# A blocked feed-forward layer with layer norm and projection: the first stage reordered with groups outermost, row means taken from a running sum, the root taken on 128x4 values, and matmul operands placed and read in one way

## The chip, the cores and the metric

One core of a Trainium2 chip. The metric is the device time of one execution in microseconds (us), the median of three runs of the kernel. One more execution was taken with the hardware profiler; all rows below are from it.

## What is computed

For x of shape 4 x 1024 x 1024 (4 batches, 1024 tokens, D = 1024 features in 8 groups of 128):

```python
xr = x.reshape(B, T, 8, 128)
h  = gelu(einsum('btel,elf->btef', xr, W1) + b1)      # W1: 8 x 128 x 512
y  = (einsum('btef,efl->btel', h, W2) + b2).reshape(B, T, D)   # W2: 8 x 512 x 128
scale, shift = split(silu(emb) @ emb_W + emb_b, 2)    # emb: 4 x 1024, emb_W: 1024 x 2048
hn = layernorm(y, ln_g, ln_b) * (1 + scale) + shift   # mean and variance over D
out = x + silu(hn) @ out_W + out_b                    # out_W: 1024 x 1024
```

All is float32. The large products are made of three matmuls in the format fp32r each: an operand is split in a rounded part ("hi") and the rest ("lo"), and hi\*hi, lo\*hi and hi\*lo are added in PSUM.

## The kernel before

**Stage A** makes y. A block is 1024 tokens (one batch), an item is one group of one block; the blocks are the outer loop (`body`, the two in the middle as a loop on the device) and the 8 groups the inner one. An item has 4 chunks of 128 hidden features. For a chunk, `first` makes six matmuls 128x128x512 (three products for two halves of the tokens) from `W` and `xT_hi`/`xT_lo` into one of two PSUM slots, the ring. ScalarE applies gelu into `g_raw` (L469), VectorE rounds to `g_hi` (L612) and subtracts to `g_lo` (L614), and `second` (six more matmuls, L792) adds into `y_psum`. TensorE issues `first` of chunk m + 2 ahead of `second` of chunk m. Per item ScalarE also rounds the next x to `xT_hi` (L465) and copies y with its bias to `y_stage` (L497), which SyncE's queue stores in `y_scratch`; VectorE makes `xT_lo` (L607). In the first block ScalarE rounds each group's W1 and W2, and GpSimd subtracts for the low parts (L387) and adds each `y_stage` to a sum for the first window (L405), in one queue. All eight groups' weights stay in SBUF. In the middle blocks ScalarE and GpSimd split out_W in the same way, and TensorE makes the eight float32 products of the conditioning (`embed`, L807).

**Stage B** works on eight windows of 512 tokens. For a window TensorE makes 4 x 48 matmuls (`project`, L892): four row tiles, eight groups, three products, two halves. Meanwhile the next window is normed: VectorE adds y over the groups and splits the sum (`group_sum`, L689 to L697), TensorE averages over partitions with a matrix of 1/D (`mean_of_sum`, L799 and L800), VectorE subtracts (L708), ScalarE squares (L565), the squares go the same way through `group_sum` and `mean_of_sum`, ScalarE takes the root and VectorE the reciprocal on 128x512 (L747), then come the product (L713), silu (L550), rounding (L719) and subtraction (L721), and after each row tile PSUM + `res` (L703). GpSimd adds `out_b` to `res` (L450), two buffers deep.

The first window is normed inside the last block of stage A: GpSimd subtracts the mean (L431), adds the squares (L436) and multiplies (L443), eight times each, and VectorE takes the reciprocal in three pieces (L669). Its silu, rounding and subtraction (`Y0_PARTS`) lie at the seam of the stages.

SBUF tensors lie behind one another, and three unused ones (`gap0`, `gap1`, `gap2`) shift them. By the declared sizes and the program's start at byte 16,512 of a partition, `W`, `oW_hi`, `oW_lo` and all `s_hi`, `s_lo` begin at byte 448 modulo 512, `xT_hi`, `xT_lo`, `g_hi`, `g_lo` at 192, `ones_r` at 352, `sum_hi` and `sum_lo` at 384. In stage A the moving operand (x or gelu) is read backwards:

```python
def from_the_end(h):
    return slice((h + 1) * BANK - 1, h * BANK - 1 if h else None, -1)
```

Of the kernel before, what the change touches and what calls it, by code (L numbers as in the profile page):

```python
# [15 lines left out]
def cond_ffn_program(nc, x, xT, vectors, W1, W2, emb_W, out_W, out_b, out):  # L16
# [5 lines left out]
    TA = T  # L22
    NA = B * T // TA
    TB = BANK
    H = TA // TB
    NB = B * T // TB
    SB = TB // P
    K = G * C
    assert L == P and D == G * L and TA == 2 * BANK and D == 2 * BANK and G % 2 == 0 and C == 4

    y_scratch = nc.dram_tensor("y_scratch", [NB, P, G, TB], F32, kind="Internal").ap()

# [10 lines left out]
    with ExitStack() as ctx:  # L43
        def sb(name, shape, dt=F32, scope=ctx):
            return scope.enter_context(nc.sbuf_tensor(name, shape, dt))
# [5 lines left out]


        sb("gap0", [P, 80])
        oW_hi = sb("oW_hi", [P, G, D], F32R)
        oW_lo = sb("oW_lo", [P, G, D], F32R)
        ident = sb("ident", [P, P])
        cols = sb("cols", [P, ROWS])
        ones_r = sb("ones_r", [P, P], F32R)
        eps = sb("eps", [P, 1])
        stat = sb("stat", [P, TB])  # L60

        sum_hi = sb("sum_hi", [P, TB], F32R)
        sum_lo = sb("sum_lo", [P, TB], F32R)
        cond_silu = sb("cond_silu", [P, KE, 32])
        cond_now = sb("cond_now", [P, 2, 32])
        emb_rows = sb("emb_rows", [P, BANK])
        sq_sum = emb_rows
        emb = sb("emb", [P, NE, B])
        mod_a = sb("mod_a", [P, B, G])
        mod_c = sb("mod_c", [P, B, G])  # L70
        mod_t = sb("mod_t", [P, B, G])
        sb("gap2", [P, 48])


        with ExitStack() as a:

            W = sb("W", [P, G, 4, FF], F32R, a)
            sb("gap1", [P, 64], F32, a)
            xT_hi = sb("xT_hi", [P, 2, TA], F32R, a)
            xT_lo = sb("xT_lo", [P, 2, TA], F32R, a)  # L80
            g_hi = sb("g_hi", [P, 2, TA], F32R, a)
            g_lo = sb("g_lo", [P, 2, TA], F32R, a)
            g_raw = sb("g_raw", [P, 2, TA], F32, a)
            xT_raw = sb("xT_raw", [P, 2, TA], F32, a)
            y_stage = sb("y_stage", [P, 2, TA], F32, a)
            wraw = sb("wraw", [P, 2, 2 * FF], F32, a)
            assert D == 2 * FF == KE * P


        with ExitStack() as b:  # L90
            yb0 = sb("yb0", [P, G, TB], F32, b)
            s_lo0 = sb("s_lo0", [P, G, TB], F32R, b)
            s_hi0 = sb("s_hi0", [P, G, TB], F32R, b)
            sq = sb("sq", [P, G, TB], F32, b)
            yb1 = sb("yb1", [P, G, TB], F32, b)
            s_hi1 = sb("s_hi1", [P, G, TB], F32R, b)
            s_lo1 = sb("s_lo1", [P, G, TB], F32R, b)
            res = sb("res", [P, 2, D], F32, b)
            out_b_all = sb("out_b_all", [P, D], F32, b)
        yb = (yb0, yb1)  # L100
        s_hi = (s_hi0, s_hi1)
        s_lo = (s_lo0, s_lo1)
        W1_HI, W1_LO, W2_HI, W2_LO = range(4)
        HG = G // 2

        squares = wraw[:].rearrange("p s (g t) -> p (s g) t", g=2)

        sp_waits = sem("sp_waits")
# [3 lines left out]
        ident_ready = sem("ident_ready")  # L112
        vec_landed = sem("vec_landed")
        ones_set = sem("ones_set")
        ones_ready = sem("ones_ready")

        wraw_landed = [sem(f"wraw_landed{s}") for s in range(2)]
        w1_landed = sem("w1_landed")
        w_hi_done = sem("w_hi_done")
        w_split0 = sem("w_split0")  # L120
# [5 lines left out]
        cond_now_ready = sem("cond_now_ready")  # L126
# [7 lines left out]
        x0_landed = [sem(f"x0_landed{h}") for h in range(2)]  # L134
        x0_hi = sem("x0_hi")
        x0_lo = sem("x0_lo")
# [4 lines left out]
        ghi_done = sem("ghi_done")  # L141
        glo_done = sem("glo_done")
        s2_done = sem("s2_done")
        y_psum_free = sem("y_psum_free")
        y_staged = sem("y_staged")
        y_stored = [sem(f"y_stored{s}") for s in range(2)]


        y0_landed = sem("y0_landed")
        y0_sum = sem("y0_sum")  # L150
        y0_split = sem("y0_split")
# [4 lines left out]
        y0_var = sem("y0_var")  # L156
        y0_std = sem("y0_std")
        y0_rstd = sem("y0_rstd")
# [7 lines left out]
        tree = sem("tree")  # L166
        sum_split = sem("sum_split")
        stat_psum = sem("stat_psum")
        centred = sem("centred")
        squared = sem("squared")  # L170
        std_done = sem("std_done")
        rstd_done = sem("rstd_done")
# [6 lines left out]
        res_landed = [sem(f"res_landed{s}") for s in range(2)]  # L179
        res_biased = sem("res_biased")  # L180
        out_ready = sem("out_ready")
        out_stored = [sem(f"out_stored{s}") for s in range(2)]


        def ring(s):
            return psum[:, 2 * s:2 * s + 2, :].rearrange("p b n -> p (b n)")

        def y_psum(s):
            return psum[:, 4 + 2 * s:6 + 2 * s, :].rearrange("p b n -> p (b n)")

        proj = [ring(0), ring(1)]
        mean_ps = psum[:, 4]
        var_ps = psum[:, 5]

        PERIOD = 16
        AT_ROUND = (2, 5)
        AT_LOAD = (6, 10)
        AT_EMB = (10, 14)
        K_EMB = [p + k for p in range(0, K, PERIOD) for k in AT_EMB]
        E_PER_BLOCK = len(K_EMB)
        K_TURN = 2
# [767 lines left out]
```

## Time and profile before

| | |
|---|---|
| median of 3 runs | 783.93 us (783.43 to 785.17) |
| the profiled execution | 777.46 us, of which the span from the first to the last instruction is 775.7 us |
| TensorE matmuls | 736.8 us busy, 95% of the span, 3172 instructions |
| VectorE | 638.9 us, 82% |
| ScalarE | 332.6 us, 43% |
| GpSimd | 215.7 us, 28% |
| DMA | 101.65 MB, mean 131 GB/s |
| granted TensorE clock | 0.998 over the span |

A matmul's record is longer than the distance to the next one (they are pipelined), so what a matmul costs is read from the distance of their starts. Idle time of the other engines counts only where TensorE waits for it.

### The profile page before, as it was taken

Reading aid. Unit: us, or ns where it says so; the run is one execution under the profiler, and the core shown is the slowest. Engines: PE = TensorE matmul, PEld = TensorE weight load, DVE = VectorE, ACT = ScalarE, POOL = GpSimd, SP = SyncE. Lnnn points to the kernel's source line nnn. Section 1 sums busy time; section 2 is a strip of 40 time slices with the busy share of each in tenths; the row PEclk is TensorE's granted clock in tenths of the full one; section 3 lists DMA queues with packets and bytes.
Section 4 is the critical chain, followed back from the end, with each engine's and each line's share of the span. In section 5 each row is a group of like instructions: output and inputs, shape, how many; then the busy total and the mean of one; then the engine's idle time right before and its main releaser. Section 6 shows DMA issues by size and latency. Waiting matters only on the chain.

```text
span 775.7 us, 8764 instructions
## 1 busy us (share of the span) xinstructions
PE 736.8 (95%) x3172; PEld 584.3 (75%) x3172; DVE 638.9 (82%) x491; ACT 332.6 (43%) x327; POOL 215.7 (28%) x107
## 2 busy tenths in 40 slices
PE   7989899999999999989988999999999999999998
PEld 5767687787787877856666878888787887878886
DVE  6898989878797887798999798989889899988511
ACT  5656466565574755556561313324131332404100
POOL 2343525022040220374342312231323121232121
PEclk9999999999999999999999999999999999999999
DMA  5343324535344443341245344242534324132321
GB/s 165 103 142 97 121 95 145 195 136 190 127 146 160 162 162 109 112 160 55 82 145 207 109 157 168 83 190 81 190 108 189 120 90 193 57 109 109 109 86 77
DMA packets 32110, 101.65 MB, mean 131 GB/s; under 512 B 2896, under 2 KB 6992, under 8 KB 29904
## 3 DMA queue, kind: packets, MB, share of 16 engines
q1 hardware_dynamic: 31408, 100.73, 36.6%
q10 hardware_dynamic: 672, 0.52, 0.2%
q8 instruction: 19, 0.31, 0.2%
q14 instruction: 11, 0.09, 0.0%
HBM read 67.69 MB, written 33.55 MB: 131 GB/s over the span
## 4 chain that ended last, share of the span: by engine, by line
PE 66%; DVE 14%; issue 13%; POOL 4%; ACT 1%; DMA 1%; SPq 0%; DVEq 0%; POOLq 0%; ACTq 0%
PE psum L892 34%; PE psum L778 14%; PE psum L792 14%; DVE g_hi L612 3%; DVE sq L689 2%; DVE sq L691 2%; DVE sum_lo L697 2%; POOL W L387 2%; PE psum L905 1%; POOL stat L405 1%; DVE g_lo L614 1%; PE psum L807 1%; DMA yb<-y_scratch 1%; DVE xT_lo L607 1%; PE psum L799 1%
## 5 line engine op out<-in xcount | busy, mean ns | idle before, releaser
L469 ACT ACTIVATE g_raw<-psum,cols 128x1024 f32<-128x1024 f32 x128 | 142.4, 1114 | 145.7 <-PE psum L778 110.6
L614 DVE TENSOR_TENSOR g_lo<-g_raw,g_hi 128x1024 fp32r<-128x1024 f32 x128 | 182.9, 1429 | 4.4
L450 POOL TENSOR_TENSOR res<-res,out_b_all 128x1024 f32<-128x1024 f32 x32 | 91.4, 2858 | 273.1 <-DMA res<-in_x 273.1
L892 PE MATMUL psum<-oW_hi,s_hi 128*128 128x512 f32 x496 | 153.4, 390 | 0.0
L892 PE MATMUL psum<-oW_lo,s_hi 128*128 128x512 f32 x496 | 153.2, 390 | 0.0
L892 PE MATMUL psum<-oW_hi,s_lo 128*128 128x512 f32 x496 | 153.2, 390 | 0.0
L778 PE MATMUL psum<-xT_hi,W 128*128 128x512 f32 x508 | 142.0, 403 | 9.6 <-POOL W L387 8.8
L612 DVE CAST g_hi<-g_raw 128x1024 fp32r<-128x1024 f32 x128 | 111.2, 869 | 41.2 <-PE psum L792 36.3
L792 PE MATMUL psum<-g_hi,W 128*128 128x512 f32 x512 | 140.8, 398 | 1.3 <-DVE g_hi L612 1.3
L778 PEld LDWEIGHTS psum<-xT_hi,W 128*128 128x128 f32 x508 | 95.0, 190 | 41.5 <-issue 18.0
L792 PEld LDWEIGHTS psum<-g_hi,W 128*128 128x128 f32 x512 | 96.0, 188 | 25.4 <-DVE g_hi L612 2.4
L892 PEld LDWEIGHTS psum<-oW_hi,s_hi 128*128 128x128 f32 x496 | 93.7, 189 | 19.7
L892 PEld LDWEIGHTS psum<-oW_lo,s_hi 128*128 128x128 f32 x496 | 93.4, 188 | 19.6
L892 PEld LDWEIGHTS psum<-oW_hi,s_lo 128*128 128x128 f32 x496 | 93.4, 188 | 19.5
L792 PE MATMUL psum<-g_lo,W 128*128 128x512 f32 x256 | 82.2, 403 | 7.5 <-DVE g_lo L614 7.3
L565 ACT ACTIVATE sq<-yb 128x2048 f32<-128x2048 f32 x14 | 26.9, 1919 | 134.7 <-DVE yb L708 134.7
L778 PE MATMUL psum<-xT_lo,W 128*128 128x512 f32 x254 | 80.7, 400 | 0.6 <-DVE xT_lo L607 0.6
L703 DVE TENSOR_TENSOR res<-psum,res 128x1024 f32<-128x1024 f32 x31 | 37.9, 1221 | 40.1 <-PE psum L892 40.1
L550 ACT ACTIVATE yb<-yb,mod_c,mod_a 128x512 f32<-128x512 f32 x64 | 47.0, 805 | 42.3 <-DVE yb L713 42.1
L792 PEld LDWEIGHTS psum<-g_lo,W 128*128 128x128 f32 x256 | 46.9, 188 | 24.0 <-DVE g_lo L614 13.8
L387 POOL TENSOR_TENSOR oW_lo<-wraw,oW_hi 128x512 f32 x16 | 29.8, 1884 | 124.7 <-ACT oW_hi L539 124.7
L778 PEld LDWEIGHTS psum<-xT_lo,W 128*128 128x128 f32 x254 | 47.9, 189 | 12.7 <-DVE xT_lo L607 1.2
(85 smaller groups left out, 598.6 us busy)
## 6 DMA issues: line engine op xcount, KB each, us to landing
y_scratch<-y_stage SPq DMA_DIRECT2D x32, 512.0 KB, 3.1
res<-in_x SPq DMA_DIRECT2D x32, 512.0 KB, 3.3
xT_raw<-in_xT SPq DMA_DIRECT2D x31, 512.0 KB, 4.7
out<-res SPq DMA_DIRECT2D x31, 512.0 KB, 2.6
yb<-y_scratch SPq DMA_DIRECT2D x7, 2048.0 KB, 8.8
wraw<-in_emb_W SPq DMA_DIRECT2D x8, 1024.0 KB, 4.8
wraw<-in_out_W SPq DMA_DIRECT2D x8, 512.0 KB, 4.6
wraw<-in_W SPq DMA_DIRECT2D x14, 256.0 KB, 3.7
```

The lines of the kernel that those rows point to most:

```text
L387: nc.gpsimd.tensor_tensor(lo, raw, hi.bitcast(F32), ALU.subtract).then_inc(pw_split, 1)
L450: nc.gpsimd.tensor_tensor(res[:, t % 2], res[:, t % 2], out_b_all[:], ALU.add).then_inc(res_biased, 1)
L469: nc.scalar.activation(g_raw[:, k % 2], ring(slot), ACT.Gelu, bias=cols[:, R_B1 + k:R_B1 + k + 1]).then_inc(gelu_done, 1)
L550: return nc.scalar.activation(yb[s][:, g], yb[s][:, g], ACT.Silu, scale=mod_a[:, b, g:g + 1], bias=mod_c[:, b, g:g + 1])
L565: nc.scalar.activation(sq[:, half], yb[s][:, half], ACT.Square).then_inc(squared, 1)
L612: nc.vector.tensor_copy(g_hi[:, s], g_raw[:, s]).then_inc(ghi_done, 1)
L614: nc.vector.tensor_tensor(g_lo[:, s], g_raw[:, s], g_hi[:, s].bitcast(F32), ALU.subtract).then_inc(glo_done, 1)
L689: nc.vector.tensor_tensor(sq[:, 0:4], src[:, 0:4], src[:, 4:8], ALU.add).then_inc(tree, 1)
L703: nc.vector.tensor_tensor(res[:, t % 2], proj[t % 2], res[:, t % 2], ALU.add).then_inc(out_ready, 1)
L778: mm = nc.tensor.matmul(ring(slot)[:, h * BANK:(h + 1) * BANK], W[:, g, w, cut], v[:, g % 2, from_the_end(h)], start=(n == 0), stop=(n == 2))
L792: mm = nc.tensor.matmul(y_psum(g % 2)[:, h * BANK:(h + 1) * BANK], W[:, g, w, cut], v[:, k % 2, from_the_end(h)], start=(c == 0 and n == 0 ...
L892: mm = nc.tensor.matmul(proj[t % 2][:, h * BANK:(h + 1) * BANK], v[:, g, cut], w[:, g, h * BANK:(h + 1) * BANK], start=(g == 0 and n == 0) ...
```

## The change

- **Order.** Stage A runs over items with the groups outside: group 0 for the four blocks, group 1 for the four, up to group 5; then for each block its groups 6 and 7. All loops are written out, none runs on the device. `W` holds three groups' weights instead of eight. The loads and splits of W and out_W are one list (`LOADS`), spread over items 0 to 22 (`PREP_ITEM`), with two splits of 512 columns on GpSimd in each such item. GpSimd no longer adds up y.
- **Means.** VectorE keeps a running sum `acc` of y over the groups for all tokens, one instruction per item (`add_up`), PSUM and `acc` in, `acc` out. The mean is one float32 matmul of `ones` with `acc`.
- **Variance and root.** The sum of squares is turned by four float32 matmuls with one column (`variance`) to 128x4, ScalarE's root and VectorE's reciprocal work on 128x4, and four transposes (`spread`) bring the result back to 128x512 in PSUM, where VectorE's product reads it. For the first window ScalarE copies it to `stat`.
- **Gelu.** Two of an item's four chunks are rounded to `g_hi` by ScalarE, right behind the gelu. In stage B the rounding of silu (`s_hi`) goes to ScalarE too.
- **Placement.** Each SBUF tensor that a matmul reads has an address that is 0 modulo 512, and all are read forward.
- `res` has four buffers instead of two; those of the first two row tiles are loaded before the last item ends. The conditioning's weights have a buffer of their own.

```diff
+    ORDER = [(g, t) for g in range(G - 2) for t in range(NT)] + [(g, t) for t in range(NT) for g in (G - 2, G - 1)]
...
+    PREP_ITEM = [None, 0, 1, 2, 3, 5, 6, 7, 9, 11, 13, 15, 17, 19, 21, 22]
...
+    Y0_MEAN_AT = (Y0_ITEM + 2, 0)
+    Y0_SQ_AT = [(Y0_ITEM + 2, 3), (Y0_ITEM + 3, 1), (Y0_ITEM + 3, 2), (Y0_ITEM + 4, 0)]
+    Y0_VAR_AT = (Y0_ITEM + 4, 3)
+    Y0_RSTD_AT = (Y0_ITEM + 5, 1)
...
+        BASE = 33 * 512
...
+    def act_rounds(m):
+        return m % C in (3, 0)
...
+                if act_rounds(m):
+                    act.wait_ge(gelu_done, m + 1)
+                    if m >= 2:
+                        act.wait_ge(s2_done, m - 1)
+                    nc.scalar.copy(g_hi[:, m % 2], g_raw[:, m % 2]).then_inc(ghi_act, 1)
...
+            def add_up(n):
+                g, t = ORDER[n]
+                dve.wait_ge(s2_done, C * n + C)
...
+                    nc.vector.scalar_tensor_tensor(acc[:, t], y_psum(n), bias, acc[:, t], ALU.add, ALU.add
+                                                   ).then_inc(acc_done, 1)
...
+            def variance(ps, sums):
+                for j in range(SB):
+                    mm = nc.tensor.matmul(ps[:, j:j + 1], sums[:, j * P:(j + 1) * P], ones[:, 0:1],
+                                          start=True, stop=True)
+                return mm
+
+            def spread(ps):
+                for j in range(SB):
+                    mm = nc.tensor.transpose(ps[:, j * P:(j + 1) * P], rstd[:, j:j + 1].to_broadcast([P, P]), ident[:])
+                return mm
...
+                at_mean, at_var, at_rstd = ((0, 3), (2, 1), (2, 5)) if i == 0 else ((0, 0), (1, 0), (1, 4))
...
+                            if i == 0:
+                                pe.wait_ge(y_staged, N)
+                                pe.wait_ge(acc_done, N)
...
+                            nc.tensor.matmul(mean_ps, ones[:], acc[:, n, (i + 1) % 2 * TB:((i + 1) % 2 + 1) * TB],
+                                             start=True, stop=True).then_inc(mean_done, 1)
...
+                            pe.wait_ge(tree, 3 * i + 3)
+                            variance(var_ps, stat).then_inc(var_done, 1)
...
-                                              v[:, g % 2, from_the_end(h)],
...
+                        mm = nc.tensor.matmul(ps[:, half], W[:, g % 3, w, cut], v[:, n % 2, half],
```

On VectorE the last `add_up` (item 31) stands behind all `Y0_PARTS`. The item of the first window's last group is item 25, so its mean stands at item 27, its squares at items 27 to 29, its variance at (29, 3) and its root at (30, 1), the second number being the chunk.

## Rows read from the trace of the kernel before

**Rows 1.** The page, part 1: busy us, share of the span, instructions.

```profile
PE 736.8 (95%) x3172; PEld 584.3 (75%) x3172; DVE 638.9 (82%) x491; ACT 332.6 (43%) x327; POOL 215.7 (28%) x107
```

**Rows 2.** Timeline, TensorE in stage A: start us, us, instruction, count.

```profile
300.89 1.10 PE L778 MATMUL psum<-xT_hi,W 128*128 128x512 f32 x4
...
303.69 1.10 PE L778 MATMUL psum<-xT_hi,W 128*128 128x512 f32 x4
```

**Rows 3.** Timeline, TensorE, start of stage B and its first mean.

```profile
403.32 0.62 PE L892 MATMUL psum<-oW_hi,s_hi 128*128 128x512 f32 x2
...
416.47 0.61 PE L892 MATMUL psum<-oW_hi,s_lo 128*128 128x512 f32 x2
420.85 0.54 PE L799 MATMUL psum<-sum_hi,ones_r 128*128 128x512 f32 x1 [3.77 <-DVE sum_lo L697]
...
421.62 1.06 PE L892 MATMUL psum<-oW_hi,s_hi 128*128 128x512 f32 x2
422.47 1.06 PE L892 MATMUL psum<-oW_lo,s_hi 128*128 128x512 f32 x2
```

**Rows 4.** The stretch behind the wait of rows 3, columns as in rows 5.

```profile
420.80:424.80 4.00, 3.95 (x10) 3.16 (x11) 2.94 (x2) 0.62 (x1) 0.00 (x0) 0.57 0.00 0
```

**Rows 5.** Stretches: us, busy (x) of PE, PEld, DVE, ACT, POOL; granted clock; DMA.

```profile
307.00:403.30 96.30, 86.53 (x353) 64.60 (x353) 87.08 (x75) 55.33 (x54) 46.02 (x25) 1.00 0.28 97
403.30:775.70 372.40, 358.17 (x1565) 294.05 (x1564) 293.93 (x175) 96.17 (x99) 91.43 (x32) 1.00 0.35 130
```

**Rows 6.** Waits of TensorE over the span: us in total, times, longest us.

```profile
PE psum L799 <- DVE sum_lo L697: 11.1, 6, 3.8
PE psum L778 <- POOL W L387: 8.8, 6, 1.6
```

**Rows 7.** Timeline, TensorE at the last wait for GpSimd's weights.

```profile
92.61 0.63 PE L792 MATMUL psum<-g_lo,W 128*128 128x512 f32 x2
94.82 0.94 PE L778 MATMUL psum<-xT_hi,W 128*128 128x512 f32 x3 [1.58 <-POOL W L387]
```

**Rows 8.** VectorE's sum of PSUM and SBUF: shortest, median, longest in ns.

```profile
L703 DVE TENSOR_TENSOR res<-psum,res x31: 1217/1220/1225, 426.3 to 761.7; 128x1024 f32<-128x1024 f32 x31
```

**Rows 9.** Groups: line, engine, operation, count, busy us, mean ns, idle before.

```profile
L469 ACT ACTIVATE g_raw<-psum,cols 128x1024 f32<-128x1024 f32 x128 | 142.4, 1114 | 145.7 <-PE psum L778 110.6
...
L465 ACT CAST xT_hi<-xT_raw 128x1024 fp32r<-128x1024 f32 x31 | 32.5, 1049 | 4.5 <-ACT y_stage L497 2.2
```

**Rows 10.** Timeline, GpSimd at the end of stage A and the seam.

```profile
380.51 15.50 POOL L443 TENSOR_TENSOR yb<-yb,stat 128x512 f32<-128x512 f32 x8 [21.84 <-DVE stat L669]
414.78 5.38 POOL L450 TENSOR_TENSOR res<-res,out_b_all 128x1024 f32<-128x1024 f32 x2 [18.77 <-DMA res<-in_x]
```

**Rows 11.** The low part of gelu, two SBUF inputs: shortest, median, longest in ns.

```profile
L614 DVE TENSOR_TENSOR g_lo<-g_raw,g_hi x128: 1224/1226/2293, 10.6 to 401.5; 128x1024 fp32r<-128x1024 f32 x128
```

**Rows 12.** Timeline, TensorE around one float32 product of the conditioning.

```profile
199.25 0.63 PE L792 MATMUL psum<-g_lo,W 128*128 128x512 f32 x2
199.81 1.07 PE L807 MATMUL psum<-wraw,cond_now 128*32 128x512 f32 x8
200.81 1.20 PE L778 MATMUL psum<-xT_hi,W 128*128 128x512 f32 x4
```

**Rows 13.** Timeline around the four float32 transposes.

```profile
306.02 0.63 PE L792 MATMUL psum<-g_lo,W 128*128 128x512 f32 x2
...
306.49 0.60 PE L855 MATMUL psum<-ident,emb_rows 128*128 128x128 f32 x4
...
306.84 0.95 PE L778 MATMUL psum<-xT_hi,W 128*128 128x512 f32 x3
```

**Rows 14.** Timeline, VectorE in a window of stage B.

```profile
556.16 4.48 DVE L708 TENSOR_TENSOR yb<-yb,psum 128x2048 f32<-128x2048 f32 x2 [0.83 <-PE psum L800]
...
566.22 0.69 DVE L693 TENSOR_TENSOR stat<-sq 128x512 f32<-128x512 f32 x1
```

**Rows 15.** Timeline, VectorE, its first work behind the seam.

```profile
411.16 2.29 DVE L689 TENSOR_TENSOR sq<-yb 128x2048 f32<-128x2048 f32 x1
```

More of the change, by code:

```diff
@@ L377, in _ @@
+            for s in range(4):
+                sp.wait_ge(out_stored[s], 16 * (QN // 4 + (s == (QN - 1) % 4)))
         @block.gpsimd
@@ new lines, in round_raw @@
+            def round_raw(j, h):
+                kind, g = LOADS[j]
+                half = slice(h * FF, (h + 1) * FF)
+                if kind == "W" and g >= 3:
+                    act.wait_ge(s2_done, C * (LAST_ITEM[g - 3] + 1))
+                landed = sum(q % 2 == j % 2 for q in range(1, j + 1))
+                act.wait_ge(wraw_landed[j % 2], 32 * landed)
+                nc.scalar.copy(W[:, g % 3, 2 * h] if kind == "W" else oW_hi[:, g, half], wraw[:, j % 2, half]
+                               ).then_inc(aw_hi_done, 1)
@@ L822, in _, with take @@
[L822 to L831 removed]
+            def take(u):
+                if u in EARLIER:
+                    kind, j = EARLIER[u]
                     if kind == "S":
[L833 removed]
+                        pe.wait_ge(gelu_done, j + 1)
@@ new lines, in take, with first @@
+                return ring(u)
+            def first(m, low_part=None):
+                n, c = divmod(m, C)
+                g = ORDER[n][0]
+                cut = slice(c * P, (c + 1) * P)
+                ps = take(("S", m))
+                for k, (w, v) in enumerate(((W1_HI, xT_hi), (W1_LO, xT_hi), (W1_HI, xT_lo))):
+                    if k == 2 and low_part is not None:
+                        pe.wait_ge(xlo_done, low_part)
+                    for h in range(2):
+                        half = slice(h * BANK, (h + 1) * BANK)
+                        mm = nc.tensor.matmul(ps[:, half], W[:, g % 3, w, cut], v[:, n % 2, half],
+                                              start=(k == 0), stop=(k == 2))
+                mm.then_inc(s1_done, 1)
@@ new lines, in second @@
+            def second(m):
+                n, c = divmod(m, C)
+                g = ORDER[n][0]
+                cut = slice(c * P, (c + 1) * P)
+                pe.wait_ge(ghi_act if act_rounds(m) else ghi_dve, ROUNDED[m])
+                for k, (w, v) in enumerate(((W2_HI, g_hi), (W2_LO, g_hi), (W2_HI, g_lo))):
+                    if k == 2:
+                        pe.wait_ge(glo_done, m + 1)
+                    for h in range(2):
+                        half = slice(h * BANK, (h + 1) * BANK)
+                        mm = nc.tensor.matmul(y_psum(n)[:, half], W[:, g % 3, w, cut], v[:, m % 2, half],
+                                              start=(c == 0 and k == 0), stop=(c == C - 1 and k == 2))
+                mm.then_inc(s2_done, 1)
```

1028 lines of the change are left out of this document (455 added, 573 removed).

## The prediction

> **What bounds the kernel now.** I read the page first: TensorE is busy for 95% of the span, VectorE for 82% [rows 1]. So the question is what one matmul costs and where TensorE is kept from the next. The timeline gives the first. In the middle of stage A twelve matmuls take 303.69 - 300.89 = 2.80 us, 233.3 ns each [rows 2]. In stage B 58 matmuls take 416.47 - 403.32 = 13.15 us, 226.7 ns each [rows 3]. There are 1536 in each stage. A floor comes from the stretch behind 421 us, where the granted clock is down: two matmuls take 422.47 - 421.62 = 0.85 us, 427 ns each, one column per pulse of 1.2 GHz [rows 3, 4]; at 2.4 GHz that is 213 ns, and no distance of these matmuls is shorter.
>
> Then the losses, from the stretches and the waits. The last two blocks of stage A, 307 to 403.3, hold 353 matmuls; at 233.3 ns they need 82.4 us of 96.3, so 13.9 us are lost there [rows 5], while VectorE is busy for 87 us and GpSimd norms the first window. In the first block TensorE waits six times for GpSimd's half of the weights, 8.8 us [rows 6]. In stage B it waits six times for the split sum, 11.1 us [rows 6]: once 3.77 us [rows 3], behind which the granted clock is 0.57 for 4.0 us, near the level of 1.2 GHz, and ten matmuls take 4.00 instead of 2.27 us [rows 4]; five times for 7.3 us in all. The reader should see that TensorE has no single bottleneck behind it, only these terms.
>
> **The change part by part**, in terms of the span of 775.7 us. The profiled execution took 777.46 us, 0.8% less than the median of 783.93; I carry the difference over to the median as it is.
>
> *Placement and direction.* In stage B the two operands begin at one byte modulo 512 (448) and are read forward: 226.7 ns. In stage A they begin at 448 and 192, and the moving one is read backwards: 233.3 ns [rows 2, 3]. Stage A gets what stage B has, so I give it stage B's distance: 1536 x 6.6 ns = 10.1 us less. Stage B stays, since it had the one place already; only the place itself moves (448 to 0). Bounds: nothing (0), and the floor of 213 ns for all 3072, which is 31 us for stage A and 21 us for stage B.
>
> The Trainium skill speaks against a gain here: "TensorE: Matmul & The Clock Gate", part 2, says that TensorE has two independent SBUF read ports and that loading the next weights takes nothing from the running matmul, so that a matmul's distance would depend on its columns alone. The two distances above, for equal columns, don't agree with it; by the rule this term would be zero and the sum 786 us.
>
> *Order of the groups.* GpSimd's share of a group's weights is now due every fourth item instead of every item, and its queue no longer holds the sum of y that stood ahead of it. The six waits go. One of them costs 94.82 - 92.61 less two distances (0.47) = 1.74 us where the wait is 1.58 [rows 7], and the matmul behind it comes 0.08 us later; so 8.8 + 6 x 0.25 = 10.3 us less. Behind it nothing else is late: GpSimd's two pieces of 1.9 us an item are few against 10.9 us.
>
> *Gelu rounding and running sum.* VectorE loses two roundings an item and gets `add_up`, which reads PSUM and one SBUF tensor like L703 and should take 1.22 us [rows 8]; its free load per item stays about 8.3 to 8.6 us of 10.9. ScalarE gets two casts of 1.05 us on top of four gelus of 1.11, y and x [rows 9]: 4.5 + 1.1 + 1.05 + 2.1 = 8.7 us, 9.9 with a weight rounding. Both hide under TensorE's 48 x 0.2267 = 10.9 us. A gelu's low part is due, counted from the end of its `first`, after four sets of six matmuls and the first four of the fifth: 5.4 + 0.9 = 6.3 us. It is ready after one set, which must have left the buffer (1.6 with the signals), a cast (1.05 and 0.1) and a subtraction (1.23): 4.0. That leaves 2.3 us, so the extra hop to ScalarE is covered too. If that cover were gone, each cast would cost what it is late.
>
> *Norming of the first window.* GpSimd still does its 23 instructions in stage A (15.50 us for eight, 1.94 each [rows 10]), and a VectorE instruction that reads two SBUF tensors then takes up to 2.29 instead of 1.23 us [rows 11], while the sum from PSUM takes 1.22 at its shortest and 1.23 at its longest [rows 8]. Before, nine VectorE instructions an item are exposed to that, now seven. The 13.9 us of rows 5 shrink by two ninths: 3.1 us less. The squares at item 28 stand close together, and ScalarE's queue can be held there by GpSimd with gelus behind it; I take that as part of what remains. TensorE's own part grows by the 2.2 us of one window, next.
>
> *Short products.* A float32 mean replaces two fp32r matmuls (0.46 us). The float32 product of the conditioning with as many columns costs 200.81 - 199.25 less two distances = 1.1 us, and 0.1 behind it [rows 12]: 1.2. Four transposes cost 306.84 - 306.02 less two distances = 0.35, and 0.1: 0.45 [rows 13]. `variance` isn't in the trace: four float32 matmuls of one column, two records each as in rows 12, hence eight weight loads. Low end: the transposes' distance, 0.35 / 4 = 0.09 us each, 0.7 and 0.1 at each side, 0.9. High end: 584.3 / 3172 = 0.18 us for a weight load [rows 1] plus a start of its own, 1.8. I take 1.5, nearer to the loads, since nothing long hides them. Per window 1.2 + 0.45 + 1.5 = 3.15 against 0.92 before: 2.2 us more, seven times 15.6 in stage B and once 2.2 in stage A.
>
> *Waits in stage B.* The five short waits go: 7.3 + 5 x 0.2 = 8.3 us less. In their place: from the mean to the end of the squares' sum VectorE and ScalarE need 566.91 - 556.16 = 10.8 us [rows 14], and `variance` stands eight groups behind the mean, 8 x 1.36 = 10.9 us. That is a tie; I take 0.3 us in each of six windows, 1.8 more (0 to 2 each, if GpSimd meets a sum). The reciprocal of 3.4 us and the slow product leave the chain, but the next window's operands were in time before, so that is worth nothing.
>
> *The seam.* Before: 420.85 - 416.47 - 0.45 = 3.9 us, and 1.7 for the clock [rows 3, 4], 5.7. After: the mean of window 1 waits for `add_up` of item 31, which VectorE does behind all of `Y0_PARTS`; these ended 411.16 - 403.32 = 7.8 us after the first projection [rows 3, 15]. Now 1.2 are added by ScalarE's last cast ahead of the silus, 1.2 by `add_up`, 0.2 for the signals, and some 3 because GpSimd's products and its first sums with `out_b`, 2.7 us each [rows 10], now fall into this stretch. That is 13.4 us, and TensorE has four groups of 1.36 to do before it: 8.0 lost, and 1.7 if the clock falls again. 9.7 - 5.7 = 4.0 more.
>
> Sum: - 10.1 - 10.3 - 3.1 + 2.2 + 15.6 - 8.3 + 1.8 + 4.0 = - 8.2 us. 783.93 - 8.2 = **775.7 us**.
>
> **The rivals.**
> 1. *The short products and the seam are cheap.* `variance` at its low end saves 0.6 x 8 = 4.8 us, GpSimd staying out of the seam and the clock staying up 4.7, the tie in stage B 1.8: 775.7 - 11.3 = 764 us. For it: loads are pulled ahead in all of stage B. Against it: one column hides no load.
> 2. *The place itself counts.* At 0 modulo 512 both stages come down toward the floor, say half of the 13.4 ns above it: 3072 x 6.7 ns = 21 us less, 755 us; the whole would be 735. For it: the rest over the floor is unexplained. Against it: 448 and 448 gave no better than 226.7.
> 3. *Slower: stage A's distance does not move.* If the 233.3 ns belong to stage A's traffic and not to place and direction, 10.1 us don't come: 775.7 + 10.1 = 786 us. It decides when the new distance is above 226.7 + 8.2 / 1.536 = 232.0 ns. For it: ScalarE and VectorE write these very tensors. Against it: the distance stays 233.3 whether they are idle or busy. (The two-port rule of "TensorE: Matmul & The Clock Gate" in the Trainium skill, part 2, would give this case.)
> 4. *Slower: the hop to ScalarE.* If the 64 casts make TensorE wait, 0.13 us each is enough to eat the gain (8.2 / 64); at 0.3 us each it is 19 us, 795 us. For it: ScalarE's queue is in order, and x, y and weights stand in it. Against it: 2.3 us of slack.
>
> **How the numbers follow.** Forecast (769 to 782): 0.42. Rival 1: 0.21. Rival 2, fully or in part: 0.11. Rival 3: 0.14. Rival 4, or the first window's chain costing as much: 0.12. A difference under 0.2% (1.6 us) can't be told from none in this kernel. Faster: all of the first three, 0.74; within 0.2%: 0.07, taken from the edges of the forecast and rival 3; slower: 0.19. The range leaves out most of rival 2 and the far half of rival 4: 757 to 789.
>
> **What the profile after would show.** Distances of 226 to 228 ns in stage A confirm the placement; 233 refute it. No wait of L778's successor for GpSimd in the first quarter. The float32 mean as two records 0.43 us apart; `variance` between 0.9 and 1.8 us from the projection before to the one behind. A gap of some 7 us in the first row tile of stage B, and a granted clock near one half behind it. VectorE's `add_up` at 1.22 us. GpSimd's squares and ScalarE waiting for its subtraction at item 28. The prediction is wrong if stage A waits steadily for ScalarE, if the variance costs over 2 us, or if the matmul distance leaves 226 to 234.

## The result, and the profile after

The kernel after the change takes 794.08 us (median of four runs, 791.87 to 795.2), the kernel before 783.68 us (782.93 to 785.17). The ratio is 1.0127, 95% interval 1.0099 to 1.0155: slower, where I had forecast 775.7 us and faster. The profiled execution took 794.72 us, with a span of 792.9. The one of the kernel before took 777.46, which is 6.2 us under that kernel's median, while this one is at its median. So the two traces lie 17.2 us apart and the medians 10.4: some 7 us of the differences between them below are no loss of the change, and nothing here says which.

The page, part 1, of the kernel after, answers to [rows 1]. VectorE has lost 150 us of work and ScalarE has gained 86, as the change intends; TensorE keeps its share of 95%, in a span that is 17 us longer.

```profile
PE 751.7 (95%) x3252; PEld 597.4 (75%) x3252; DVE 489.3 (62%) x393; ACT 418.1 (53%) x413; POOL 165.6 (21%) x91
```

The timeline of TensorE in stage A answers to [rows 2]. From the first of these two lines to the last are twelve matmuls: 153.46 - 150.74 = 2.72 us, 226.7 ns each, where it was 233.3.

```profile
150.74 1.07 PE L682 MATMUL psum<-xT_hi,W 128*128 128x512 f32 x4
...
153.46 1.07 PE L682 MATMUL psum<-xT_hi,W 128*128 128x512 f32 x4
```

The waits of TensorE over the span, as in [rows 6]:

```profile
PE psum L682 <- DVE xT_lo L525: 13.4, 11, 4.4
PE psum L728 <- DVE W L512: 5.8, 1, 5.8
PE psum L822 <- DVE acc L548: 4.5, 1, 4.5
PE psum L682 <- ACT g_raw L400: 2.6, 2, 1.6
PE psum L696 <- DVE g_lo L537: 2.2, 3, 1.0
PE psum L778 <- DVE res L608: 1.9, 1, 1.9
PE psum L682 <- ACT stat L462: 1.8, 1, 1.8
PE psum L778 <- DVE s_hi L599: 1.8, 1, 1.8
PE psum L778 <- DVE s_lo L601: 1.6, 1, 1.6
```

The reader should see that both waits of [rows 6] are gone, the six for GpSimd's weights and the six for `sum_lo`, and that a new one leads the list: eleven times TensorE waits for `xT_lo`, the low part of the next item's input. The wait for `W` at L728 is the start of the kernel, which was there before.

To find where the time went I cut each trace at three points of TensorE's timeline: its first matmul, the mean of the first window, and the first projection. In each piece I count the 512-column matmuls of the two layers and of the projection, and take off 226.7 ns for each. What is left is the loss of the piece; for the kernel before, the longer distance of stage A counts as loss here. "Predicted" applies the terms of the prediction to the losses of the kernel before: 31.9 - 7.9 - 10.3, then 17.4 - 2.2 - 3.1 + 2.2, then 24.1 + 15.6 - 8.3 + 1.8 + 4.0.

| us | first matmul | first mean | first projection | span | loss to the mean | mean to projection | stage B |
|---|---|---|---|---|---|---|---|
| before | 5.8 | 309.7 (1200 matmuls) | 403.3 (336) | 775.7 | 31.9 | 17.4 | 24.1 |
| predicted | | | | 767.5 | 13.7 | 14.3 | 37.2 |
| after | 5.8 | 328.6 (1308) | 408.0 (228) | 792.9 | 26.3 | 27.8 | 36.7 |

Stage B is where I had put it, 12.6 us worse against 13.1 predicted. Stage A should have gained 21.3 us (49.3 to 28.0) and lost 4.8 (54.1): between these traces the whole miss is there, 12.6 us ahead of the mean and 13.5 behind it. In medians the miss is 18.4 us (794.08 against 775.7).

A part of the two losses behind the first mean is the clock. In the kernel after, the granted clock is 0.50, which is the level of 1.2 GHz, in five stretches of 27 us together (columns as in [rows 5]):

```profile
338.30:341.70 3.40, 3.40 (x10) 2.62 (x9) 0.73 (x1) 1.26 (x2) 0.00 (x0) 0.50 0.00 0
369.00:379.20 10.20, 9.39 (x26) 7.74 (x27) 4.31 (x4) 3.44 (x4) 0.00 (x0) 0.50 0.00 0
410.00:416.80 6.80, 6.01 (x14) 4.75 (x15) 6.70 (x8) 0.21 (x1) 2.39 (x2) 0.50 0.42 161
423.60:427.00 3.40, 3.40 (x9) 2.34 (x8) 2.59 (x2) 0.27 (x1) 0.00 (x0) 0.50 0.91 381
468.00:471.40 3.40, 3.40 (x8) 1.98 (x7) 0.50 (x2) 0.00 (x0) 0.00 (x0) 0.50 1.00 288
```

Fifty of the long matmuls (512 columns) start in them. Each takes 427 ns there instead of 226.7, so by this estimate the slow clock costs 10.0 us, 5.2 between mean and projection and 4.8 in stage B. In the kernel before it is one stretch, 421.1 to 424.5, with seven of them, 1.4 us. The prediction had put the clock at 1.7 us, in the seam alone.

### The profile page after: what moved, and what is told of

Its sections match the earlier page's. It is cut to its first block, busy times and chain, and to the rows that moved or that the text cites. A ratio compares the mean times of both kernels' runs of the same rounds, so it can differ in the third digit from the quotient of the medians.

```text
span 792.9 us, 8091 instructions
## 1 busy us (share of the span) xinstructions
PE 751.7 (95%) x3252; PEld 597.4 (75%) x3252; DVE 489.3 (62%) x393; ACT 418.1 (53%) x413; POOL 165.6 (21%) x91
## 4 chain that ended last, share of the span: by engine, by line
PE 78%; DVE 11%; ACT 5%; issue 4%; DMA 2%; POOL 1%; SPq 0%; ACTq 0%; DVEq 0%; POOLq 0%
PE psum L778 39%; PE psum L682 17%; PE psum L696 17%; DVE g_lo L537 4%; DVE xT_lo L525 2%; DVE g_hi L535 2%; PE psum L789 1%; ACT g_raw L400 1%; DMA xT_raw<-in_xT 1%; PE psum L711 1%; PE psum L822 1%; PE psum L704 1%; DVE s_hi L599 1%; ACT yb L470 1%; ACT xT_hi L392 1%
## 5 line engine op out<-in xcount | busy, mean ns | idle before, releaser
L537 DVE TENSOR_TENSOR g_lo<-g_raw,g_hi 128x1024 fp32r<-128x1024 f32 x128 | 178.3, 1393 | 74.1 <-ACT g_hi L406 71.9
L778 PE MATMUL psum<-oW_hi,s_hi 128*128 128x512 f32 x496 | 159.7, 403 | 3.7 <-DVE res L608 1.9
L778 PE MATMUL psum<-oW_hi,s_lo 128*128 128x512 f32 x496 | 155.2, 394 | 1.6 <-DVE s_lo L601 1.6
L682 PE MATMUL psum<-xT_hi,W 128*128 128x512 f32 x508 | 140.0, 398 | 5.0 <-ACT g_raw L400 2.6
L381 POOL TENSOR_TENSOR res<-res,out_b_all 128x1024 f32<-128x1024 f32 x32 | 79.0, 2472 | 281.6 <-DMA res<-in_x 281.6
L682 PE MATMUL psum<-xT_lo,W 128*128 128x512 f32 x254 | 82.4, 406 | 13.4 <-DVE xT_lo L525 13.4
L696 PE MATMUL psum<-g_lo,W 128*128 128x512 f32 x256 | 80.2, 395 | 2.2 <-DVE g_lo L537 2.2
L406 ACT CAST g_hi<-g_raw 128x1024 fp32r<-128x1024 f32 x64 | 67.2, 1050 | 22.4 <-PE psum L696 22.3
L535 DVE CAST g_hi<-g_raw 128x1024 fp32r<-128x1024 f32 x64 | 47.2, 738 | 22.7 <-ACT g_raw L400 17.0
L696 PEld LDWEIGHTS psum<-g_lo,W 128*128 128x128 f32 x256 | 48.5, 190 | 13.8 <-DVE g_lo L537 3.5
```

Of the source, the lines that this page charges most:

```text
L381: nc.gpsimd.tensor_tensor(res[:, q % 4], res[:, q % 4], out_b_all[:], ALU.add).then_inc(res_biased, 1)
L406: nc.scalar.copy(g_hi[:, m % 2], g_raw[:, m % 2]).then_inc(ghi_act, 1)
L535: nc.vector.tensor_copy(g_hi[:, m % 2], g_raw[:, m % 2]).then_inc(ghi_dve, 1)
L537: nc.vector.tensor_tensor(g_lo[:, m % 2], g_raw[:, m % 2], g_hi[:, m % 2].bitcast(F32), ALU.subtract).then_inc(glo_done, 1)
L682: mm = nc.tensor.matmul(ps[:, half], W[:, g % 3, w, cut], v[:, n % 2, half], start=(k == 0), stop=(k == 2))
L696: mm = nc.tensor.matmul(y_psum(n)[:, half], W[:, g % 3, w, cut], v[:, m % 2, half], start=(c == 0 and k == 0), stop=(c == C - 1 and k == 2))
```

## The experiments

**The subtraction of `xT_lo` one chunk earlier.** The waits name `xT_lo`. These are the lines of VectorE's timeline ahead of one of them, in the kernel after, then TensorE's, ScalarE's and GpSimd's:

```profile
24.53 1.23 DVE L537 TENSOR_TENSOR g_lo<-g_raw,g_hi 128x1024 fp32r<-128x1024 f32 x1
26.26 0.69 DVE L535 CAST g_hi<-g_raw 128x1024 fp32r<-128x1024 f32 x1 [0.50 <-ACT g_raw L400]
26.99 2.20 DVE L537 TENSOR_TENSOR g_lo<-g_raw,g_hi 128x1024 fp32r<-128x1024 f32 x1
29.11 1.21 DVE L525 TENSOR_TENSOR xT_lo<-xT_raw,xT_hi 128x1024 fp32r<-128x1024 f32 x1
```

```profile
28.40 1.07 PE L682 MATMUL psum<-xT_hi,W 128*128 128x512 f32 x4
30.37 0.73 PE L682 MATMUL psum<-xT_lo,W 128*128 128x512 f32 x2 [0.91 <-DVE xT_lo L525]
```

```profile
24.18 1.04 ACT L392 CAST xT_hi<-xT_raw 128x1024 fp32r<-128x1024 f32 x1
```

```profile
26.81 1.29 POOL L348 TENSOR_TENSOR W<-wraw,W 128x512 fp32r<-128x512 f32 x1 [2.86 <-ACT W L415]
```

ScalarE has `xT_hi` at 25.22, but VectorE takes the subtraction up only at 29.11, behind the rounding of the item's third chunk, and ends it at 30.32. TensorE has done its four `xT_hi` matmuls by then and starts at 30.37. The low part ahead of it takes 2.20 us instead of 1.23, beside GpSimd's subtraction for the weights; the 0.97 us more are as much as the wait of 0.91. So it is the place in the queue and GpSimd's work next to it that make `xT_lo` late here. The kernel before had `rest_xT` at chunk 0 of an item; the diff has it at chunk 1, one gelu later in the queue. The edit puts it back:

```diff
-                if c == 1 and n + 1 < N:
+                if c == 0 and n + 1 < N:
                     rest_x(n + 1)
```

> The changed kernel with one move: VectorE makes an item's xT_lo one chunk earlier, as the kernel before did. Theory A (a deadline that my prediction overlooked: xT_lo is due 0.9 us into the third chunk's matmuls, but stands behind a low part of gelu that waits for its turn): the waits of TensorE for xT_lo, 13.4 us in the changed kernel, go nearly all, and the time falls by 10 to 15 us, to 779 to 784 us. Rival (the wait only changes its name, since VectorE or ScalarE is the bound in stage A): the time falls by less than 3 us and waits for g_hi or g_lo take its place.

Measured: 776.28 us against 777.76 for the kernel before on that chip, ratio 0.9963, interval 0.9938 to 0.9989; the span is 775.5 us, 17.4 less than after. These are single executions; by the two ratios to the kernel before, 1.0127 and 0.9963, the gain is 1.6%, some 13 us, within the 10 to 15 us expected. The loss to the mean falls from 26.3 to 15.2 us and the one behind it from 27.8 to 21.3; stage B keeps its 36.9. In VectorE's timeline the subtraction now stands in front of the same rounding, and the wait is down to one:

```profile
23.80 1.23 DVE L537 TENSOR_TENSOR g_lo<-g_raw,g_hi 128x1024 fp32r<-128x1024 f32 x1
24.94 1.22 DVE L525 TENSOR_TENSOR xT_lo<-xT_raw,xT_hi 128x1024 fp32r<-128x1024 f32 x1
26.07 0.69 DVE L535 CAST g_hi<-g_raw 128x1024 fp32r<-128x1024 f32 x1
```

```profile
PE psum L682 <- DVE xT_lo L525: 0.6, 1, 0.6
```

So one line of the queue's order is worth some 13 us by the ratios and 17.4 us between the two traces, and the rest of the rewrite is about even with the kernel before: its ratio of 0.9963 lies within the range of the forecast, though not at its middle. The slow clock isn't what the move gives back: 44 long matmuls still start at 0.50 (8.8 us by the same estimate).

**No rounding by ScalarE.** Rival 4 of the prediction said that the hop to ScalarE costs.

```diff
     def act_rounds(m):
-        return m % C in (3, 0)
+        return False
```

> The changed kernel with all roundings of gelu on VectorE, none on ScalarE. If the hop to ScalarE is what makes VectorE late for xT_lo (it waits for ScalarE's cast 71.9 us in all), the waits for xT_lo fall and the time falls by 3 us or more. If the hop is harmless, VectorE, which then has nine instructions an item that read SBUF alone and add_up besides, loses more where GpSimd works: slower by 3 us or more.

Measured: 797.22 us against 777.76, ratio 1.0244 (1.0195 to 1.0293), span 793.9. The loss to the mean is 32.1 us (26.3 after), behind it 28.8, in stage B 30.7 (36.7). `xT_lo` is still waited for, ten times, 11.6 us. The hop isn't the cause: ScalarE's roundings save stage A 6.8 us. They cost stage B 6.0; there the wait for `acc` is 2.4 us instead of 4.5, and what the rest is wasn't taken apart. By the ratios this kernel is slower than the one after by 1.2%, which its span (1.0 us more) doesn't show.

**GpSimd's part of the first norming cut down.** In the first window GpSimd subtracts, sums and multiplies 512 columns; this kernel leaves out all but 8 of them in each instruction except the first sum. The sums are cut in the same way as the two lines shown.

```diff
-nc.gpsimd.tensor_tensor(yb0[:, g], yb0[:, g], stat[:], ALU.subtract)
+nc.gpsimd.tensor_tensor(yb0[:, g, 0:8], yb0[:, g, 0:8], stat[:, 0:8], ALU.subtract)
...
-nc.gpsimd.tensor_tensor(yb0[:, g], yb0[:, g], stat[:], ALU.mult)
+nc.gpsimd.tensor_tensor(yb0[:, g, 0:8], yb0[:, g, 0:8], stat[:, 0:8], ALU.mult)
```

> Leaves out work: GpSimd's subtractions, products and all but the first of its sums for the first window are done on 8 columns of 512, so that window's norm is not computed; the order and the signals stay. Theory B (GpSimd's chain for the first window, with ScalarE's squares waiting in their queue for it and VectorE held by it, costs most of the 28 us that the stretch from the window's mean to the first projection loses): that loss falls under 12 us. Rival (the loss is the late xT_lo and the table loads): it stays above 20 us.

Measured: span 776.2 us, one run of 777.96. The loss to the mean stays (27.5), the one from the mean to the projection falls from 27.8 to 12.2 us, stage B from 36.7 to 34.1. That is just above the 12 us expected, and far from the rival's 20. So more than half of what is lost there comes with the time of GpSimd's instructions, in its chain and in what they do to VectorE, and not with TensorE's own short products, which are unchanged. Of the 15.6 us, some 5.2 are the slow clock, which doesn't fall between mean and projection in this run. The timeline of the kernel after shows the worst of it. First GpSimd, then ScalarE, VectorE and TensorE:

```profile
354.88 5.99 POOL L367 TENSOR_TENSOR yb<-yb,stat 128x512 f32<-128x512 f32 x4
360.82 7.85 POOL L372 TENSOR_TENSOR emb_rows<-emb_rows,squares 128x512 f32<-128x512 f32 x4
```

```profile
358.44 1.06 ACT L453 ACTIVATE squares<-yb 128x1024 f32<-128x1024 f32 x1 [3.90 <-POOL yb L367]
359.40 1.10 ACT L400 ACTIVATE g_raw<-psum,cols 128x1024 f32<-128x1024 f32 x1
```

```profile
365.39 2.17 DVE L537 TENSOR_TENSOR g_lo<-g_raw,g_hi 128x1024 fp32r<-128x1024 f32 x1
367.48 2.28 DVE L525 TENSOR_TENSOR xT_lo<-xT_raw,xT_hi 128x1024 fp32r<-128x1024 f32 x1
```

```profile
369.81 1.22 PE L682 MATMUL psum<-xT_lo,W 128*128 128x512 f32 x2 [4.43 <-DVE xT_lo L525]
```

ScalarE stands 3.90 us in front of a square whose input GpSimd still centres, with a gelu queued behind it. VectorE's next rounding is then late, its subtractions beside GpSimd's sums take 2.2 us instead of 1.23, `xT_lo` stands behind them, and TensorE waits 4.43 us. The stretches of the kernel after (columns as in [rows 5]) show the clock that this costs:

```profile
352.00:384.00 32.00, 24.67 (x90) 18.72 (x89) 17.69 (x14) 18.39 (x19) 16.08 (x10) 0.84 0.10 34
384.00:406.00 22.00, 17.64 (x73) 13.13 (x72) 16.18 (x12) 15.14 (x16) 16.22 (x9) 1.00 0.44 167
406.00:430.00 24.00, 16.14 (x48) 11.63 (x47) 21.10 (x14) 7.20 (x8) 10.10 (x4) 0.79 0.51 197
```

Around and behind this wait the granted clock is 0.50 from 369.0 to 379.2, as shown above: TensorE runs at 1.2 GHz for 10.2 us. With `xT_lo` repaired no wait of that length is left here, and the clock is down for as long all the same, from 353.0 to 363.2, behind waits of 1.61, 0.60, 0.56 and 0.95 us.

**The norming given more items.** Besides the earlier subtraction, groups 5, 6 and 7 go block by block at the end instead of 6 and 7, so the first window is complete four items earlier and its norming has eleven items instead of seven. One load of `PREP_ITEM` moves from item 21 to 20 with it.

```diff
-    ORDER = [(g, t) for g in range(G - 2) for t in range(NT)] + [(g, t) for t in range(NT) for g in (G - 2, G - 1)]
+    ORDER = [(g, t) for g in range(G - 3) for t in range(NT)] + [(g, t) for t in range(NT) for g in (G - 3, G - 2, G - 1)]
...
-    Y0_SQ_AT = [(Y0_ITEM + 2, 3), (Y0_ITEM + 3, 1), (Y0_ITEM + 3, 2), (Y0_ITEM + 4, 0)]
-    Y0_VAR_AT = (Y0_ITEM + 4, 3)
-    Y0_RSTD_AT = (Y0_ITEM + 5, 1)
+    Y0_SQ_AT = [(Y0_ITEM + 2, 3), (Y0_ITEM + 3, 1), (Y0_ITEM + 4, 2), (Y0_ITEM + 5, 0)]
+    Y0_VAR_AT = (Y0_ITEM + 6, 0)
+    Y0_RSTD_AT = (Y0_ITEM + 6, 3)
```

> Besides the earlier xT_lo subtraction, groups 5, 6 and 7 instead of 6 and 7 go block by block at the end, so the first window's mean comes four items earlier and its norming has eleven items left instead of seven (the squares spread over more chunks, the variance and the reciprocal later). Span of the run with only the earlier subtraction: 775.5 us, of which 21.3 us lost against 226.7 ns per matmul between the mean and the first projection, and 36.9 us after it. Theory (this loss is the norming chain through GpSimd run against its deadlines, and its last tail of GpSimd multiplications that collides with the last items and the silus): the 21.3 us shrink to about 8 to 12, and the seam gains 0 to 3 us because the sums of out_b with x then come earlier; span 761 to 768. Rival (the loss is inherent work of the chain on TensorE, ScalarE and VectorE: short products, activation tables, copies): it stays within 3 us of 21.3 and the span above 772.

Measured: 765.3 us against 781.35, ratio 0.9827 (0.978 to 0.9873), span 763.0. Between the mean and the projection, now over 372 matmuls, 13.0 us are lost (21.3 with the early subtraction alone), and stage B loses 32.8 (36.9), 4.1 less where I had allowed for 3. The first is a little more than expected, but far nearer to the theory than to its rival: the same work in more items loses 8.3 us less. Some 3.4 of them are the slow clock, which no longer falls between mean and projection.

**The mean of window 1 one row tile later.** In the kernel after, TensorE waits 4.50 us at the first mean of stage B for the last `add_up`.

```diff
-                at_mean, at_var, at_rstd = ((0, 3), (2, 1), (2, 5)) if i == 0 else ((0, 0), (1, 0), (1, 4))
+                at_mean, at_var, at_rstd = ((1, 0), (2, 3), (2, 7)) if i == 0 else ((0, 0), (1, 0), (1, 4))
```

> The changed kernel with window 1's mean behind the first group of the second row tile (1, 0), its variance at (2, 3) and its root at (2, 7). Theory C (the seam loses because the mean stands where the last add_up can't be ready): the wait of 4.9 us and the slow clock behind it, about 2 us more, go, and the span falls by 5 to 7 us unless window 1's second half comes later. Rival (the chain behind the mean is as late as before and only the place of the wait changes): the wait comes back at the variance or at the start of window 1, and the span falls by under 2 us.

Measured: span 788.7 us, one run of 790.47. Stage B loses 35.6 us, only 1.1 less than after; the other 3.1 us of span lie ahead of the first projection, where this kernel is the same as the one after. The wait for `acc` is gone from the list; the one for `res` has grown from 1.9 us to 7.1 us, in two waits. So a later mean mostly hands the wait on, as the rival said; that it is VectorE's whole queue that is late is argued here, and the next run tests it.

**VectorE's queue in the seam put in order.** VectorE's timeline at the seam of the kernel after, and GpSimd's under it:

```profile
405.37 1.27 DVE L548 SCALAR_TENSOR_TENSOR acc<-psum,cols,acc 128x1024 f32<-128x1024 f32 x1
406.57 1.38 DVE L599 CAST s_hi<-yb 128x512 fp32r<-128x512 f32 x1
407.99 2.75 DVE L601 TENSOR_TENSOR s_lo<-yb,s_hi 128x512 fp32r<-128x512 f32 x1
...
411.11 0.69 DVE L601 TENSOR_TENSOR s_lo<-yb,s_hi 128x512 fp32r<-128x512 f32 x1
...
415.44 2.87 DVE L599 CAST s_hi<-yb 128x1024 fp32r<-128x1024 f32 x1
418.35 3.25 DVE L601 TENSOR_TENSOR s_lo<-yb,s_hi 128x1024 fp32r<-128x1024 f32 x1
421.52 1.27 DVE L548 SCALAR_TENSOR_TENSOR acc<-psum,cols,acc 128x1024 f32<-128x1024 f32 x1
```

```profile
404.33 5.85 POOL L381 TENSOR_TENSOR res<-res,out_b_all 128x1024 f32<-128x1024 f32 x2
414.60 5.91 POOL L381 TENSOR_TENSOR res<-res,out_b_all 128x1024 f32<-128x1024 f32 x2 [4.41 <-DMA res<-in_x]
```

The last running sum, on which the mean waits, stands last, behind two instructions that take 2.87 and 3.25 us beside the sums with `out_b`, instead of 0.69 and 1.23. Besides the earlier `xT_lo`, this kernel moves it up, rounds the last chunk on VectorE, and brings variance and rstd forward:

```diff
-        return m % C in (3, 0)
+        return m % C in (3, 0) and m != M - 1
...
             for n, part in enumerate(Y0_PARTS):
+                if part.start == HG:
+                    dve.wait_ge(y_staged, N)
+                    add_up(N - 1)
                 dve.wait_ge(y0_silu, part.stop)
...
-            add_up(N - 1)
...
-                at_mean, at_var, at_rstd = ((0, 3), (2, 1), (2, 5)) if i == 0 else ((0, 0), (1, 0), (1, 4))
+                at_mean, at_var, at_rstd = ((0, 3), (1, 4), (2, 0)) if i == 0 else ((0, 0), (1, 0), (1, 4))
```

> Besides the earlier xT_lo subtraction, the last chunk of gelu is rounded by VectorE instead of ScalarE, the last running sum is put before the third-to-last part of the first window's s_hi and s_lo in VectorE's queue (behind the last y_stage of ScalarE), and the variance and the rstd of the next window come at row tile 1 group 4 and row tile 2 group 0 instead of row tile 2 groups 1 and 5. Span of the run with only the earlier subtraction: 775.5 us, of which 36.9 us lost after the first projection, its window 0 60.2 us long. Theory (the mean matmul behind row tile 0 group 3 waits for the last running sum, which stands last in VectorE's queue, and window 1 starts late because everything behind that mean is late): the gap of about 5.8 us on TensorE there goes to below 1.5, window 0 takes 50 to 55 us, window 1 about 46.5, and the span is 764 to 770. Rival (VectorE's and GpSimd's total work in the seam bounds it, whatever its order): the wait moves to s_hi or s_lo or to the finish of row tiles, window 0 and 1 together gain less than 2 us, span above 773.

Measured: 770.15 us against 781.35, ratio 0.9881 (0.9836 to 0.9926), span 764.7. The profiled execution is the fastest of the four; the others have spans of 767.7 to 769.1. Stage B loses 26.1 us instead of 36.9; window 0 takes 50.9 us (60.2) and window 1 46.2 (47.6). The wait for `acc` is gone; 1.7 us appear in front of the variance. The same two instructions are still as long beside GpSimd, but nothing is due behind them. Which of the edit's three parts gives how much wasn't taken apart:

```profile
393.83 1.28 DVE L548 SCALAR_TENSOR_TENSOR acc<-psum,cols,acc 128x1024 f32<-128x1024 f32 x1
...
396.88 2.88 DVE L602 CAST s_hi<-yb 128x1024 fp32r<-128x1024 f32 x1
399.80 3.29 DVE L604 TENSOR_TENSOR s_lo<-yb,s_hi 128x1024 fp32r<-128x1024 f32 x1
```

**Place and direction, taken apart in the kernel before.** One kernel gives stage A's operands one place modulo 512 (448 and 448), another reads the moving operand forward at the old places (192 and 448), a third does both. Forward is the second edit, one place the first:

```diff
-            sb("gap1", [P, 64], F32, a)
...
-return slice((h + 1) * BANK - 1, h * BANK - 1 if h else None, -1)
+return slice(h * BANK, (h + 1) * BANK)
```

> The kernel before with the gap of 256 bytes taken away, so that stage A's moving operands begin at 448 modulo 512 as its weights do, and read forward. Theory (place and direction alone set the distance): stage A's matmul distance goes from 233.3 to 226.7 ns and the time falls by 8 to 10 us. Rival (the distance belongs to the rewritten order): it stays at 233.3 ns.

> The kernel before with the gap of 256 bytes taken away alone: all operands at 448 modulo 512, the moving one of stage A still read backwards. If only the place counts: 226.7 ns. If direction counts: the distance is above 233 ns, since reading backwards from the same place meets the weights' reads.

> The kernel before read forward alone: weights at 448, moving operands at 192 modulo 512. If only direction counts: 226.7 ns. If the place counts too: above 230 ns, by the 236 ns that the kernel before shows where a load from byte 352 follows a product from byte 448.

Measured: one place and backwards, span 778.3 us and one run of 780.13, a distance of 233.3 ns; forward at two places, span 772.4 and 774.23, 226.7 ns; both, 772.46 against 778.37, ratio 0.9923 (0.9894 to 0.9951), span 771.4, 226.7 ns. TensorE's timeline gives each distance over twelve matmuls, first one place and backwards, 253.02 - 250.22 = 2.80 us:

```profile
250.22 1.10 PE L777 MATMUL psum<-xT_hi,W 128*128 128x512 f32 x4
...
253.02 1.10 PE L777 MATMUL psum<-xT_hi,W 128*128 128x512 f32 x4
```

then forward at two places, 252.71 - 249.99 = 2.72 us:

```profile
249.99 1.07 PE L778 MATMUL psum<-xT_hi,W 128*128 128x512 f32 x4
...
252.71 1.07 PE L778 MATMUL psum<-xT_hi,W 128*128 128x512 f32 x4
```

The direction is the whole effect on the distance and the place none; nor is it above 233.3 ns at one place, as I had expected if the two reads met. The time falls by less than the 8 to 10 us expected: 0.77%, some 6 us (3.8 to 8.3 by the interval). The 10.1 us that shorter distances free don't all arrive: to the first mean the losses go from 31.9 to 25.9 us, 6.0 where 1200 x 6.6 ns are 7.9, and behind it they stay at 17.5, where 2.2 were due. A faster TensorE meets the same deadlines sooner: the waits for GpSimd's weights grow from 8.8 [rows 6] to 10.2 us, and those for `g_lo` from 7.3 to 8.8.

**All three repairs together.** The earlier `xT_lo`, the order of groups and the seam.

> The earlier xT_lo subtraction, the earlier norming of the first window and the new order of the seam, all together. If the three losses are separate, their gains add: from 792.9 (span of the changed kernel) -17.4 (measured for the first) -9 to -13 (norming) -6 to -11 (seam) gives 752 to 760, median time 753 to 761, which would be faster than the kernel before (783.7) by 3%. If the norming and the seam compete for the same GpSimd and VectorE time, only the larger of the two gains shows: 764 to 768.

Measured: 760.03 us (759.01 to 763.09, six runs) against 781.35, ratio 0.975, interval 0.9713 to 0.9786; span 758.5. The losses are 15.3, 12.7 and 28.4 us. Relative to the early subtraction alone the norming had brought 12.5 us of span and the seam 10.8, and together it is 17.0, which looks as if the two shared 6 us. But the seam's execution was a fast one of its kernel. By the ratios the gains are 1.4%, 0.8% and together 2.1%, which add up, each within some 0.5%; whether they share anything isn't resolved. The expectation of added gains, 753 to 761 us, holds. This version beats the kernel before by 2.5%, and the one after by 3.7% by the ratios (4.3% between the two spans). With 11 long matmuls at the slow clock it loses 2.2 us there instead of 10.0.

## Why the prediction was wrong

*What failed first: the step "Gelu rounding and running sum".* It reckoned VectorE's load per item and the due time of the gelu's low part, and concluded that all of it hides. It gave no due time to `xT_lo`, which stands in the same queue and which the diff moves from chunk 0 to chunk 1, behind a subtraction that GpSimd's splits of the weights lengthen. The load was right (196.5 us in the 249 from 76 to 325, 8.6 an item), the order was not read. The price is some 13 us by the ratios and 17.4 us of span between the traces, 11.1 ahead of the mean and 6.5 behind it, of a miss of 18.4 in the medians. With the subtraction back in place, the loss ahead of the mean is 15.2 us against 13.7 predicted, which bears out the two large gains of the sum together. None of the three signs of being wrong that the prediction named came up: stage A doesn't wait steadily for ScalarE, the variance stays under 2 us, and the distance is 226.7 ns. A sign for `xT_lo` was missing as its due time was.

*"Norming of the first window" was mis-sized.* I scaled the loss by the number of VectorE instructions that GpSimd can stretch, nine to seven, and got 14.3 us for the stretch. It is 21.3 once `xT_lo` is repaired. The instructions are as slow as I read them (2.2 us); what I had named and then set at nothing is the chain itself, ScalarE held 3.90 us by GpSimd with gelus behind it; and the clock I had not reckoned here at all, at 0.50 for 13.6 us. The run with short GpSimd instructions (12.2 us) and the run with more items (13.0 us) show that either cure works, against 27.8 and 21.3 us without it. How the rest splits between the chain and the stretched instructions wasn't measured by itself.

*Placement and direction.* The distance came out as forecast, 226.7 ns, and rival 3 is out: stage A's own traffic doesn't hold it at 233.3. The cause that I named was half wrong, since place doesn't enter. Rival 2 is out with it: at 0 modulo 512 stage B keeps 226.7. So the two-port rule of "TensorE: Matmul & The Clock Gate" in the Trainium skill, part 2, was weighed wrongly by me: the two distances that I held against it differ by the direction of reading and not by the loading of weights, so they say nothing against what the page states of loading. What fails is my conclusion from it, that a distance depends on its columns alone. In terms of time the term of 10.1 us is an upper bound; in the kernel before it was worth some 6 us (ratio 0.9923), since waits take a part back.

*Order of the groups.* Right: the six waits are gone.

*Short products and waits in stage B.* Oversized. Windows 3 to 6 take 46.1 us each, 43.5 of them projection, so 2.6 us for all short products and waits, where I had 3.15 + 0.3. TensorE's timeline shows the variance: from the last projection's line ahead of it to the one behind are 575.88 - 574.37 = 1.51 us, less two distances 1.06 us, where I took 1.5.

```profile
574.37 0.61 PE L778 MATMUL psum<-oW_hi,s_lo 128*128 128x512 f32 x2
574.97 1.05 PE L711 MATMUL psum<-ones,stat 128*128 128x1 f32 x8
575.88 0.71 PE L778 MATMUL psum<-oW_hi,s_hi 128*128 128x512 f32 x2
```

These windows cost no more than before (46.2 us each), where my terms added 0.9 to each.

*The seam.* Undersized by about as much. Windows 0 and 1 went from 96.5 us to 107.6, 11.1 more; my terms gave them some 7. The mechanism was the one predicted, the mean behind `add_up` behind all of `Y0_PARTS`, and its wait of 4.5 us was even shorter than the 8.0 forecast. What I left out are the waits around it, `s_lo` in the first projection (1.6 us, behind 1.8 for `s_hi` just ahead of it) and `res` at window 1 (1.9), and a clock that falls three times in stage B instead of once, 4.8 us by the estimate above where I had 1.7. That stage B comes out at 36.7 us against 37.2 is two errors that cancel, not a confirmation of the terms.

*Rival 4* gave nearly the measured time, 795 us, for a reason that the run without ScalarE's roundings refutes: it is no faster (span 793.9). That its number fits is luck. The other half of its chance, the first window's chain, is a true part of the loss.

## What to carry to other kernels

When an in-order queue is rewritten, write down the due time of every instruction in it, the unchanged ones too, and compare the place of each with the old queue: a free third of the engine did not save one instruction that came one chunk late. A helper engine's chain costs by its deadlines as much as by its busy time, so giving it slack in items can bring as much as making it shorter (13.0 and 12.2 us lost here); and put in front of the queue what the bounding engine waits for. Compare versions by the ratios of several executions, and use two single traces to find a place and not to price it: here the two traces put some 7 us more between the kernels than the medians do. A stage total that matches the forecast proves little until its windows are read one by one.

## What the runs showed of the hardware

- Reading a moving operand of 512 fp32r columns backwards costs 6.6 ns a matmul (233.3 against 226.7), at one place modulo 512 and at two.
- A VectorE instruction with an input in PSUM was not stretched by GpSimd in this kernel: `add_up` takes 1.27 us at 405.37 while GpSimd's sums run from 404.33 to 410.18 (1.27 to 1.28 in all its 28 instances), and the `s_lo` at 407.99, which begins in the same time, takes 2.75 us, 0.69 when GpSimd is idle (411.11). A cast with one SBUF input is stretched too, 0.69 to 2.87. The Trainium skill, in "SBUF — State Buffer", "SBUF: two separate sides", has VectorE and GpSimd share one pair of ports, which one of them holds for a whole instruction. The trace agrees as far as the added 2.1 us are less than one GpSimd sum of 2.9.
- The granted clock fell to 0.50 (1.2 GHz) around TensorE's longest waits: for 10.2 us at the one of 4.43 (369.0 to 379.2) and for 3.4 at the one of 4.50 (423.6 to 427.0), as behind 3.77 in the kernel before [rows 4]. It fell for 3.4 us behind waits of 1.9 us too (338.3 and 468.0), and with `xT_lo` repaired for 10.2 us behind four waits of 0.56 to 1.61 us. So the longest wait alone doesn't tell how long the clock stays down; what else does, these runs don't show.
